# Weights instead of tokens held in TensorE, in the shared expert and the expert jobs of a mixture-of-experts block

## What is computed

```python
x = x + 0.5 * ffn(layernorm(x))
x = x + attention(layernorm(x))
x = x + 0.5 * ffn(layernorm(x))
```

```python
scores = softmax(xt @ router_w + router_b) + router_bias      # 16 experts in 4 groups
# the 2 best groups, in them the 2 best experts; gate = their scores
h = silu(xt @ w1[e] + b1[e]) * (xt @ w2[e] + b2[e])           # 512 -> 128
y = sum over the 2 experts: gate[e] * (h @ w3[e] + b3[e])     # 128 -> 512
z = silu(xt @ sw1 + sb1) * (xt @ sw2 + sb2) @ sw3 + sb3       # shared expert, 512 -> 256 -> 512
return y + z
```

## Time and profile before

| | |
|---|---|
| median of 3 runs | 502.72 us (501.08 to 503.02) |
| the profiled execution | 500.1 us, its span 498.3 us |
| PE busy | 438.6 us, 88% of the span |
| PE weight loads | 261.6 us, 52% |
| DVE busy | 257.5 us, 52% |
| POOL busy | 167.8 us, 34% |
| ACT busy | 153.2 us, 31% |
| mean granted clock of PE | 0.97 of full |
| DMA | 65.5 MB, 131 GB/s |

### The profile page before, as it was taken

How to read it: one execution, slowest core, us unless ns; L and a number is a source line. 1 busy time by engine, 2 the same in 40 slices (tenths; PEclk the granted TensorE clock), 3 DMA queues, 4 the chain that set the end, 5 groups by cost and what they waited for, 6 DMA issues and landing times.

```text
span 498.3 us, 7954 instructions
## 1 busy us (share of the span) xinstructions
PE 438.6 (88%) x2540; PEld 261.6 (52%) x2541; DVE 257.5 (52%) x723; ACT 153.2 (31%) x316; POOL 167.8 (34%) x234
## 2 busy tenths in 40 slices
PE   1899969999998998889998998989989789999990
PEld 1534346676635766556654653436434366667530
DVE  5465712222249965888866866332387403222337
ACT  0511112323211322256643644734221113232210
POOL 1801124555323752344332422520000215555410
PEclk9999989999998999999999999899999969999996
DMA  7999924433369569232221000101200123433377
GB/s 233 321 345 315 307 87 125 151 109 121 109 235 363 147 154 197 57 105 72 68 73 44 25 5 1 68 22 43 86 0 0 43 64 127 148 102 129 106 263 285
DMA packets 48837, 65.50 MB, mean 131 GB/s; under 512 B 6756, under 2 KB 28156, under 8 KB 48762
## 3 DMA queue, kind: packets, MB, share of 16 engines
q1 hardware_dynamic: 40277, 42.61, 27.0%
q0 software_dynamic: 6528, 19.72, 12.5%
q10 hardware_dynamic: 2000, 2.76, 1.9%
HBM read 47.66 MB, written 19.82 MB: 135 GB/s over the span
## 4 chain that ended last, share of the span: by engine, by line
PE 67%; DVE 11%; issue 10%; DMA 6%; ACT 3%; SPq 1%; ACTq 0%; POOLq 0%; POOL 0%; DVEq 0%
PE ps L1397 16%; PE ps L1410 6%; PE ps L1255 6%; PE ps L1566 6%; PE ps L1481 5%; PE ps L1538 4%; PE ps L1383 4%; PE ps L1510 2%; DVE arena L1100 2%; PE ps L1306 2%; PE ps L1395 2%; DMA q_dram<-arena 2%; PE ps L1524 2%; PE ps L1512 2%; PE ps L1548 2%
## 5 line engine op out<-in xcount | busy, mean ns | idle before, releaser
L1397 PE MATMUL ps<-w,arena 128*128 x304 | 80.5, 410 | 0.0
L1100 DVE TENSOR_REDUCE arena<-ps 128x3 f32<-128x384 f32 x128 | 67.1, 550 | 15.4 <-PE ps L1512 14.3
L600 POOL TENSOR_SCALAR_AFFINE_SELECT arena<-arena 128x512 f32<-128x512 f32 x64 | 41.0, 641 | 82.0 <-ACT arena L740 81.7
L740 ACT ACTIVATE arena<-ps 128x768 f32<-128x768 f32 x64 | 51.7, 812 | 49.7 <-PE ps L1526 49.0
L1397 PEld LDWEIGHTS ps<-w,arena 128*128 128x128 f32 x304 | 57.8, 200 | 12.0 <-issue 0.8
L527 POOL DMA_INDIRECT arena<-xn_dram,arena x40 | 39.0, 976 | 71.7 <-issue 45.4
L1255 PE MATMUL ps<-turns,arena 128*128 128x512 f32 x128 | 59.6, 596 | 0.0
L532 POOL DMA_INDIRECT y_dram<-arena x38 | 38.5, 1013 | 49.0 <-DVE arena L1010 45.9
L1004 DVE TENSOR_TENSOR arena<-ps,arena 128x128 f32<-128x128 f32 x38 | 11.1, 292 | 83.5 <-ACT arena L666 48.8
L1010 DVE COPY arena<-ps 128x512 f32<-128x512 f32 x36 | 24.9, 692 | 32.0 <-PE ps L1410 28.4
L666 ACT ACTIVATE arena<-ps 128x128 f32<-128x128 f32 x38 | 10.6, 278 | 97.6 <-PE ps L1397 97.6
(11 more groups left out here) (188 smaller groups left out, 624.5 us busy)
## 6 DMA issues: line engine op xcount, KB each, us to landing
arena<-y_dram SPq DMA_DIRECT2D x16, 512.0 KB, 7.4
arena<-q_dram SPq DMA_DIRECT2D x36, 128.0 KB, 2.7
xn_dram<-arena SPq DMA_DIRECT2D x16, 256.0 KB, 3.1
w<-in_L_ffn_ew_dram SPq DMA_DIRECT2D x4, 1024.0 KB, 9.8
q_dram<-arena SPq DMA_DIRECT2D x16, 192.0 KB, 2.8
x<-_attn_hidden_states_dram SPq DMA_DIRECT2D x4, 512.0 KB, 6.2
out_dram<-x SPq DMA_DIRECT2D x8, 256.0 KB, 3.5
turns<-in_L_ffn_sw_dram ACTq DMA_DIRECT2D x3, 512.0 KB, 6.5
```

Source lines behind the costliest of these rows:

```text
L740: act.activation(pr[:, n % 2, pair, :], ps[:, bank:bank + 2, :].rearrange("p a b -> p (a b)")[:, 0:768], ACT.Exp).then_inc(sem("exp"), 1)
L1100: dve.tensor_reduce(m3[:, h:h + 1, :], ps[:, bank, 0:3 * P].rearrange("p (n k) -> p n k", n=3), AX_X, ALU.max).then_inc(sem("s_max"), 1)
L1397: ins = pe.matmul(o, xgT[:, par, c, :], w12[:, ds(e, 1), c, :], start=False, stop=(c == KC - 1))
```

## The change

**Operands of `up`.** In the jobs and in the shared expert the weights become the stationary operand and the turned tokens are streamed, so that h comes out already turned. The turns of h and ACT's copies of them go. In the jobs there are 8 products of 128 columns instead of 4 of 256; in the shared expert two tiles go together, 8 products of 256 columns for each half of the hidden width.

**Biases.** The biases of h are now one number per partition: ACT adds the first within silu, DVE the second within the gating. The bias products go, and with them the splitting of biases on POOL and their way over memory. For the jobs PE makes columns `ebj` of biases with two small products per pass (`job_biases`), from a comparison on DVE.

**Fixed place.** ACT copies each job's weights `w1`, `w2` (128 x 1024 elements) from `w12` to one of two buffers `wj`, so that PE's operand has a fixed address.

**Order.** PE now turns the rows of job j+1 ahead of the `up` of job j, so they are ready one whole `up` before they are used; `down` of j-1 follows. The ranks, gates and the list take other places between the shared tiles. In the last stage DVE takes two tiles of pairs before the shared tile 6.

**Waits for weights.** Each group of 4 experts has a semaphore of its own. In the first pass the first three jobs wait only for the groups that they use (`need`), job 3 for all.

```diff
-            sp.dma_start(b12f[0:E, 0:INTER], eb1).then_inc(sem("bias_in"), 16)
-            sp.dma_start(b12f[0:E, INTER:2 * INTER], eb2).then_inc(sem("bias_in"), 16)
-            sp.dma_start(b12f[E:E + 1, :], sb1.rearrange("(a d) -> a d", a=1)).then_inc(sem("bias_in"), 16)
-            sp.dma_start(b12f[E + 1:E + 2, :], sb2.rearrange("(a d) -> a d", a=1)).then_inc(sem("bias_in"), 16)
-
-            sp.wait_ge(sem("bias_split"), 5)
-            sp.dma_start(b12_dram.rearrange("k e f -> e k f"), b12p).then_inc(sem("bias_out"), 16)
+            sp.dma_start(eb[:, 0:INTER], eb1).then_inc(sem("bias_in"), 16)
+            sp.dma_start(eb[:, INTER:], eb2).then_inc(sem("bias_in"), 16)
             experts_in(sp, 0, 1)
-            sp.wait_ge(sem("bias_out"), 16)
-            sp.dma_start(b12x[:], b12_dram.rearrange("k e f -> k (e f)")).then_inc(sem("bias_out"), 16)
...
-                act.activation(sg[:, par, 0:INTER], ps[:, PS_GU + par, 0:INTER], ACT.Silu).then_inc(sem(f"silu{f}"), 1)
-
-            def h_copy(j, par):
-                act.wait_ge(sem(f"ht{f}"), j + 1)
-                act.copy(hT[:, par, 0:INTER], ps[:, PS_HT, P * par:P * par + P]).then_inc(sem(f"hT{f}"), 1)
-
-            def body(j, par):
-                silu(j + 1, 1 - par)
-                h_copy(j, par)
-                gather_copy(j + 2, par)
+                act.activation(sg[:, par, 0:INTER], ps[:, PS_GU + par, 0:P], ACT.Silu, bias=ebj[:, 0, ds(j, 1)]).then_inc(sem(f"silu{f}"), 1)
+
+            def weights_copy(j, par, e):
+                if not (type(j) is int and j < 2):
+                    act.wait_ge(sem(f"gu{f}"), j - 1)
+                act.copy(wj[:, par].rearrange("p c f -> p (c f)"), w12[:, ds(e, 1)].rearrange("p a c f -> p (a c f)")).then_inc(sem(f"wj{f}"), 1)
+
+            def expert(j):
+                return act.value_load(jex[0:1, ds(j, 1)], min_val=0, max_val=E - 1)
+
             act.wait_ge(sem("jex"), f + 1)
             rest = act.value_load(jm[:], min_val=JOBS_LEAST // 2 - AHEAD, max_val=JOBS // 2 - AHEAD)
+            first = [expert(j) for j in range(3)]
+            if f == 0:
+
+                act.wait_ge(sem("need"), 1)
+                counts = [act.value_load(need[0:1, g - 1:g], min_val=1, max_val=49) for g in range(1, E // EG)]
+                act.wait_ge(sem("ew_in0"), 48)
+                for g in range(1, E // EG):
+                    act.wait_ge(sem(f"ew_in{g}"), counts[g - 1])
+            weights_copy(0, 0, first[0])
+            weights_copy(1, 1, first[1])
+            act.wait_ge(sem("job_bias"), f + 1)
+            act.copy(ebj[:].rearrange("p n j -> p (n j)"), ps[:, PS_HT, 0:2 * JP]).then_inc(sem("ebj"), 1)
             gather_copy(0, 0)
+            gather_copy(1, 1)
+            act.wait_ge(sem("ebj"), f + 1)
             silu(0, 0)
-            gather_copy(1, 1)
-            body(0, 0)
-            body(1, 1)
+            gather_copy(2, 0)
+            weights_copy(2, 0, first[2])
+            if f == 0:
+                for g in range(1, E // EG):
+                    act.wait_ge(sem(f"ew_in{g}"), 49)
             with act.Fori(0, rest + 1) as i:
-                body(2 * i + 2, 0)
-                body(2 * i + 3, 1)
-            h_copy(2 * rest + 4, 0)
+                e3 = expert(2 * i + 3)
+                silu(2 * i + 1, 1)
+                gather_copy(2 * i + 3, 1)
+                weights_copy(2 * i + 3, 1, e3)
+                e4 = expert(2 * i + 4)
+                silu(2 * i + 2, 0)
+                gather_copy(2 * i + 4, 0)
+                weights_copy(2 * i + 4, 0, e4)
+            silu(2 * rest + 3, 1)
+            silu(2 * rest + 4, 0)
             shared(FIRST, NT)
 
...
 
                 dve.wait_ge(sem("s_silu"), NT * f + t + 1)
-                dve.tensor_tensor(hh[:, t % 2, :], ps[:, PS_GU + t % 2, SHARED:], sg[:, t % 2, :], ALU.mult).then_inc(sem("s_h"), 1)
+                if f == 0 and t == 0:
+                    dve.wait_ge(sem("shb_in"), 32)
+                if t >= 4:
+                    dve.wait_ge(sem("s_z"), NT * f + 2 * (t // 2) - 2)
+                dve.scalar_tensor_tensor(out=hidden[t // 2 % 2][:, t % 2, :], in0=ps[:, PS_GU + t % 2, SHARED:],
+                                         scalar=shb[:, 1, t % 2:t % 2 + 1], in1=sg[:, t % 2, :],
+                                         op0=ALU.add, op1=ALU.mult).then_inc(sem("s_h"), 1)
...
+                for t in range(2):
+                    pairs_x(t)
                 shared_x(6)
-                for t in range(NT - 1):
+                for t in range(2, 6):
                     pairs_x(t)
                 shared_x(7)
+                pairs_x(6)
                 pairs_x(7)
             return pairs_x, shared_h, shared_x
...
-        def shared_up(f, t, chunks):
+        def shared_up(f, t):
             pe = nc.tensor
-            o = ps[:, PS_GU + t % 2, :]
-            if 0 in chunks and t >= 2:
+            pair, half = t // 2, t % 2
+            if t >= 2:
                 pe.wait_ge(sem("s_h"), NT * f + t - 1)
-            for c in chunks:
-                pe.matmul(o, xnT[:, t, c, :], sw12[:, c, :], start=(c == 0), stop=False)
-            if KC - 1 in chunks:
-                if f == 0 and t == 0:
-                    pe.wait_ge(sem("bias_out"), 32)
-                pe.matmul(o, ones[0:3, :], b12x[:, E * 2 * INTER:], start=False, stop=True).then_inc(sem("s_gu"), 1)
+            for part in range(2):
+                cols = slice(part * SHARED + half * P, part * SHARED + half * P + P)
+                o = ps[:, PS_GU + half, part * SHARED:(part + 1) * SHARED].rearrange("p (t q) -> p t q", t=2)
+                for c in range(KC):
+                    ins = pe.matmul(o, sw12[:, c, cols], xnT[:, 2 * pair:2 * pair + 2, c, :], start=(c == 0), stop=(c == KC - 1))
+            ins.then_inc(sem("s_gu"), 1)
 
...
+                if f == 0:
+                    pe.wait_ge(sem("bias_in"), 32)
+                pe.wait_ge(sem("of_job"), f + 1)
+                for n in range(2):
+                    ins = pe.matmul(ps[:, PS_HT, n * JP:(n + 1) * JP], eb[:, n * INTER:(n + 1) * INTER], of_job[:], start=True, stop=True)
+                ins.then_inc(sem("job_bias"), 1)
+
+            for t in range(FIRST):
+                if not (f == 1 and t < EARLY):
+                    shared_up(f, t)
+                if t == 2 and f == 1:
+                    pe.wait_ge(sem("wo_in"), 32)
+                if t == 4 and f == 1:
+                    gates()
+                if t >= 2:
+                    shared_down(t - 2)
+                if t == 2 + f:
+                    ranks()
+                if t == 3 and f == 0:
+                    gates()
+                if t == 4 + f:
+                    listing()
+            biases((0, 1))
+            shared_down(4)
+            shared_down(5)
+            biases((2,))
+            job_biases()
             if f == 0:
-                pe.wait_ge(sem("ew_in"), 16 * 3 * E // EG)
+                pe.wait_ge(sem("ew_in0"), 48)
             pe.wait_ge(sem("jex"), f + 1)
...
                 pe.wait_ge(sem(f"xgT{f}"), j + 1)
+                pe.wait_ge(sem(f"wj{f}"), j + 1)
                 if before is not None:
                     pe.wait_ge(sem(f"h{f}"), before)
-                o = ps[:, PS_GU + par, 0:2 * INTER]
-                pe.matmul(o, ones[0:3, :], b12x[:, ds(e * 2 * INTER, 2 * INTER)], start=True, stop=False)
-                for c in range(KC):
-                    ins = pe.matmul(o, xgT[:, par, c, :], w12[:, ds(e, 1), c, :], start=False, stop=(c == KC - 1))
+                for n in range(2):
+                    o = ps[:, PS_GU + par, n * P:(n + 1) * P]
+                    for c in range(KC):
+                        ins = pe.matmul(o, wj[:, par, c, n * INTER:(n + 1) * INTER], xgT[:, par, c, :], start=(c == 0), stop=(c == KC - 1))
                 ins.then_inc(sem(f"gu{f}"), 1)
 
-            def h_turn(j, par):
+            def down(j, par, e, before=None):
                 pe.wait_ge(sem(f"h{f}"), j + 1)
-                if not (type(j) is int and j < 1):
-                    pe.wait_ge(sem(f"hT{f}"), j)
-                pe.transpose(ps[:, PS_HT, P * par:P * par + P], hh[:, par, 0:INTER], ident).then_inc(sem(f"ht{f}"), 1)
-
-            def down(j, par, e, before=None):
-                pe.wait_ge(sem(f"hT{f}"), j + 1)
                 if before is not None:
                     pe.wait_ge(sem(f"y_sb{f}"), before)
-                pe.matmul(ps[:, PS_Y + par, :], hT[:, par, 0:INTER], w3[:, ds(e, 1), :], start=True, stop=True).then_inc(sem(f"y{f}"), 1)
+                pe.matmul(ps[:, PS_Y + par, :], hT[:, par, 0:P], w3[:, ds(e, 1), :], start=True, stop=True).then_inc(sem(f"y{f}"), 1)
 
             pe.wait_ge(sem("biased"), BIASED * (f + 1))
+            if f == 0:
+
+                pe.wait_ge(sem("need"), 1)
+                counts = [pe.value_load(need[0:1, g - 1:g], min_val=1, max_val=49) for g in range(1, E // EG)]
+                for g in range(1, E // EG):
```

(24 more changed lines are left out.)

176 lines of the change are left out of this document (73 added, 103 removed).

## The result

The changed kernel takes **467.5 us** (median of 4 runs, 466.3 to 469.5) against 502.9 (501.1 to 503.2) for the kernel before, run beside it: ratio 0.931, 95% interval 0.926 to 0.935. The profiled execution took 466.35 us with a span of 464.6, where before it was 500.1 and 498.3. The forecast was 465, faster.

A forecast was written before the change was run, and what follows sets the result against it. TensorE's own queue was taken to bound both job stages. Terms -4.5 - 11.4 + 1 - 6.0 - 13.4 - 2.7 = -37.0 against profiled 500.1 (median 502.72) gave 463 or 466, stated as 465 us; range 456 to 480.

The forecast's parts named there:

- The job: One expert job on TensorE in both job loops: 3.09 us instead of 3.54 to 3.61.
- 0.44, 1.79, 0.86: TensorE's us per job: 0.44 turning, 1.79 `up` (16 passes at 0.112), 0.86 `down`.
- Both rivals on loads: `up` in both job loops: loads not hidden, 0.215 per pass, 528 us, chance 0.04; half hidden, 0.163, 496 us, chance 0.05.
- First job stage: First pass's job loop: 71.4 us becomes 58.5, with 1.5 kept for half clock; -11.4 us.
- Second job stage: Second pass's job loop: 73.9 us becomes 58.5, plus 2 for the clock; -13.4 us.
- The 2 us I kept for the clock: Second job stage: allowance for a clock that may fall again, full loss about 4, none if shorter idle avoids it.
- First head: Start up to the first `up`: first turn near 60.3, first `up` near 61.7 against 66.17; -4.5 us.
- three register loads ... I take 0.55: First head, between VectorE's last bias sum and the first turn: each load estimated at 0.55 us with its register work.
- First tail: End of the first pass: between +0.4 and +5 us (both `down` at half clock), taken as +1.
- Attention: Attention stage between first tail and second head: no term in the sum, forecast change 0.
- Second head: Before the second job stage: list about 6 us earlier, first `up` near 392.0 against 397.98; -6.0 us.
- Second tail: End of the second pass: two pairs on VectorE come before shared tile 6; -2.7 us.

The follow-up runs named there:

- repeated run: The changed kernel run once more with nothing altered, to see which stage lengths repeat; 466.6 us, ratio 0.929.
- the fills: Changed kernel with register loads before the bias-sum wait, h of tile 7 before the first pair, unread TensorE products in first-pass idle time; 464.7 us, ratio 0.926.
- late pairs: Changed kernel, but in the last tail VectorE adds pairs of tiles 0 and 1 behind shared tile 6, as before the change; 467.0 us, ratio 0.930.

## Why the prediction was right, and where not

The time came out 2.5 us above the forecast. Some of that closeness is luck: the stages missed by +1.5, +0.3, -0.9, +2.1, +0.2, -1.3 and +1.4, and those with opposite signs cancel in part.

**The job (3.09 forecast, 3.08 to 3.09 measured).** All of its terms hold: 0.44, 1.79, 0.86. Both rivals on loads fall, by the timeline (0.112 per pass), and the experiments show why: load (0.112) and stream (0.108) are nearly equal at this width and run at the same time. Both job stages came within 1.3 us.

**First job stage (-11.4, measured -11.1).** The clock fell for 3.4 us as allowed.

**Second job stage (-13.4, measured -14.7).** The 2 us I kept for the clock were not needed. PE waited 0.64, 0.69 and 0.67 us at the turns around the first `up`, no longer in one piece, and the clock stayed at 1.00:

```profile
380.00:383.00 3.00, 2.33 (x21) 2.15 (x20) 0.19 (x1) 0.95 (x2) 1.26 (x2) 1.00 0.47 124
383.00:400.00 17.00, 17.00 (x125) 14.37 (x126) 5.37 (x11) 10.48 (x17) 9.65 (x10) 1.00 0.44 147
```

Before, 10.2 us there were at 0.50.

**First head (-4.5, measured -3.0).** The step that was mis-sized is "three register loads ... I take 0.55": they are 0.64 to 0.69 apart, and the turn follows the last by 0.85, so 2.2 instead of 1.65. The rest is that the bias sums end at about 59.6 instead of 58.6, and that moves from execution to execution: with the same code the first of the three loads starts between 58.2 and 60.6, and the first `up` follows it by 3.5 to 4.0 each time. So of the miss only the part of the loads is sure. It matters less than it looks, since an earlier first turn meets the third gather.

**First tail (+1, measured +0.1).** PE stood 2.8 us where I had 3.4, and the clock stayed at 1.00. That was the lucky case: in five of the nine traces with this code it fell there, as the term allowed, and the tail was 1.8 to 3.2 us longer than before. The one drop that the stage had beside it before (154.3 to 157.7, at the start of attention) went as well.

**Attention (0, measured +2.1; +1.3 repeated, +2.0 with the fills).** This step failed: I took a stage that the change does not touch as one that keeps its length. Two things moved, as PE's instructions show when set against the same ones of before. Up to the first products of q attention had *gained* 1.5 us, since the drop of the clock at 154.3 was gone; by the product that stood at 199.21 before, most of it is lost again (1.2 to 2.0 us in the three executions). There PE waits for scores that need q, written to memory and read back. Before:

```profile
199.21 0.28 PE L1510 MATMUL ps<-cb 128*128 128x256 bf16 x1 [1.22 <-DVE arena L1100]
```

and the same product in the run with the fills, and what stood in front of it in that run's chain of waits (start, us, what):

```profile
182.54 0.28 PE L1547 MATMUL ps<-cb 128*128 128x256 bf16 x1 [2.52 <-DVE arena L1138]
```

```profile
175.83 5.21 DMA q_dram<-arena
181.12 0.38 ACT arena L723
181.59 0.42 DVE arena L1129
182.02 0.46 DVE arena L1138
```

PE came 1.3 us sooner and waited 1.3 us more. (In the repeated run a part of this wait lies at 162, in front of a turn, behind a transfer of 3.8 us.) In the run with h of tile 7 first, where the half clock came back to the start of attention (6.8 us), the first products of q were 2.9 us later than in these three executions, and by this product 1.0 or less was left of it. So this wait takes up what PE gains or loses before it.

Right before the transfer that ends the wait, the chain has not PE but a row of DMA issues by SP, six of 0.57 to 0.63 us and a seventh. The end of that row and the transfer, before the change and in the changed kernel's own trace (start, us, what):

```profile
190.67 0.78 SPq L314
191.50 6.21 DMA q_dram<-arena
```

```profile
175.41 0.63 SPq L380
176.08 0.63 SPq L380
176.76 0.61 SPq L318
177.41 6.05 DMA q_dram<-arena
```

Counted from the start of the stage the transfer starts at 38.7 us before (191.50 - 152.84) and at 38.6 after (177.41 - 138.85); over all traces it is 38.3 and 38.7 before and 38.6 to 40.1 after. The 1.5 us that PE had gained did not bring the transfer forward. No run made SP's issues fewer or moved them, so what would bring it forward is not tested.

Second, just behind it, between 200 and 218 of before, 0.8 us are lost where the clock falls once (repeated run; also the kernel before without its bias product) and 2.2 to 2.4 where it falls twice (changed kernel, fills, late pairs); before it did not fall there. All thirteen traces fit: what this stretch lost was 0 with no drop, 0.8 to 1.4 us with one of 3.4, 2.2 to 2.4 with two, 3.8 with one of 3.4 and one of 6.8, 4.7 with two of 6.8. So the clock as the cause has much for it, but no run took the drops away, and why they come here after the change and did not before stays open.

**Second head (-6.0, measured -5.8).** Right.

**Second tail (-2.7, measured -1.3; -2.8 when repeated; -1.3 to -2.9 in ten traces with the new order).** DVE's part was right (last pair 21.2 after the last `down`, from 23.9). I had left out the stores behind it.

The Trainium skill's list (TensorE: Matmul & The Clock Gate, what overlaps and what doesn't), named in the prediction, would have no load overlap with matmuls of the same rows. The runs go on disagreeing: 16 loads and 16 streams take 1.79 together, not the 3.44 of no overlap.

## What to carry to other kernels

Count a TensorE pass as the longer of its stream and its weight load: here the operand swap was nearly free at 128 columns of f32, with narrower streams the load sets the pass, and the gain came from the bias product, the turn and the waits it made needless. A copy that feeds TensorE also waits for what stands before it in its own engine's queue; here one position of the turn in PE's order was worth 1.05 to 1.2 us per job. Where an early stage gets faster, look for the next transfer behind it before counting the gain: the first head's further gain and that at the start of attention were both given back. And before a miss of a microsecond or two in one stage is explained, look whether the stage repeats.

## What was not expected of the hardware

Copies on ACT that follow one another overlap: 128 elements last 0.30 each and start 0.20 apart, 256 last 0.41 and four take 1.32. The half clock came for 3.4, 6.8 or 10.2 us around the first head and the first jobs, beside PE's idle time, in all twelve traces without fills; in the one trace with products that nobody reads put into that time it stayed at 1.00. The same store at the end took 2.5 to 3.8 us behind DVE's last operation. And the profile's releaser can be wrong by its own rule: the wait put down to the weights was one for three register loads.
